# A fused two-layer mixture kernel on one core: phases of 3, 3 and 2 batches in the second mixture, and the second expert bias added once per batch

## What is computed

```python
x = x + 0.5 * L0_ffn(layernorm(x))     # mixture 1: top 2 of 8 experts per token
x = x + L0_attn(layernorm(x))          # 16 causal heads of 8 features, rotary
x = x + 0.5 * L0_ffn(layernorm(x))     # mixture 2, the same weights
x = x + 0.5 * L1_ffn(layernorm(x))     # 6-bit quantized 128x128 product + bias
x = x + L1_attn(layernorm(x))          # gated causal scan, then gated feed-forward
x = x + 0.5 * L1_ffn(layernorm(x))     # as above

# L0_ffn: combine[e] is the softmax gate of expert e for the token, 0 for six of the eight
h = relu(x @ w1 + bb1)                 # 128 -> 512
acc = acc + (h @ w2 + bb2) * combine[e]
```

## Time and profile before

| | |
|---|---|
| median of 3 runs | 953.89 us |
| the profiled execution | 953.64 us, of which the span from first to last instruction is 951.9 us |
| mean granted TensorE clock | 0.948 of full speed |
| busy of the span | PE 89%, DVE 64%, ACT 58%, POOL 70% |
| DMA | 127.65 MB, 134 GB/s |

### The profile page before, as it was taken

The page is one execution under the profiler, slowest core; times in us unless marked ns, Lnnn a source line. Parts: engine busy times, 40 slices in busy tenths (PEclk is TensorE's granted clock), DMA queues, the critical chain, the costliest instruction groups (busy, mean ns, idle before and its releaser), DMA issues.

```text
span 951.9 us, 23220 instructions
## 1 busy us (share of the span) xinstructions
PE 843.4 (89%) x7513; PEld 612.7 (64%) x7513; DVE 612.6 (64%) x1906; ACT 551.4 (58%) x1230; POOL 662.0 (70%) x846
## 2 busy tenths in 40 slices
PE   6379899989999999999999999999987998756894
PEld 3279798837665765665566655559965997344563
DVE  7620255674687977788979777865435335588775
ACT  4345444365568666675776667575763557735752
POOL 3789785998864378597734986971899874886432
PEclk8679899999999999998999999999999999878897
DMA  8878576736553434533443543325533771101000
GB/s 310 293 228 249 166 207 193 224 108 182 168 162 94 119 118 144 143 105 103 122 135 107 146 141 98 112 65 156 156 95 97 219 210 56 28 26 33 1 12 33
DMA packets 116280, 127.65 MB, mean 134 GB/s; under 512 B 14779, under 2 KB 84667, under 8 KB 116038
## 3 DMA queue, kind: packets, MB, share of 16 engines
q1 hardware_dynamic: 107974, 109.38, 39.4%
q0 software_dynamic: 8192, 16.79, 5.9%
HBM read 85.35 MB, written 40.39 MB: 132 GB/s over the span
## 4 chain that ended last, share of the span: by engine, by line
PE 41%; POOL 29%; DVE 15%; issue 7%; ACT 5%; DMA 2%; POOLq 0%; DVEq 0%; ACTq 0%
PE bank L801 38%; POOL z_scratch L1700 9%; POOL small L1691 9%; POOL yg L1713 4%; PE bank L813 4%; DVE sm_m L1324 3%; ACT P L1575 2%; POOL P L1735 2%; POOL sm_f L1675 1%; DMA yg<-y_scratch,pos 1%; DVE xs L1265 1%; POOL sm_p L1675 1%; DVE sm_f L1146 1%; POOL xs L1771 1%; ACT P L1488 1%
## 5 line engine op out<-in xcount | busy, mean ns | idle before, releaser
L1324 DVE TENSOR_REDUCE sm_m<-bank 128x4 f32<-128x512 f32 (+2 forms) x320 | 204.5, 683 | 37.8 <-PE bank L801 37.0
L1575 ACT ACTIVATE P<-bank 128x512 f32<-128x512 f32 x320 | 175.9, 601 | 60.1 <-PE bank L801 55.6
L801 PE MATMUL bank<-w2r,hb 128*128 x1360 | 188.0, 282 | 0.0
L801 PE MATMUL bank<-zt,wt 128*128 128x128 f32 x1360 | 182.9, 285 | 4.6 <-ACT zt L1518 2.9
L801 PEld LDWEIGHTS bank<-zt,wt 128*128 128x128 f32 x1360 | 167.3, 197 | 17.9 <-ACT P L1575 5.0
L1735 POOL TENSOR_SCALAR_AFFINE_SELECT P<-P 128x256 f32<-128x256 f32 (+1 forms) x320 | 115.5, 377 | 90.5 <-ACT P L1575 86.8
L801 PEld LDWEIGHTS bank<-w2r,hb 128*128 128x128 f32 x1360 | 165.6, 192 | 3.4 <-issue 1.6
L1700 POOL DMA_INDIRECT z_scratch<-zb,pos x128 | 134.2, 1048 | 45.7 <-issue 25.8
L1534 ACT ACTIVATE hb<-bank 128x512 f32<-128x512 f32 x170 | 101.3, 597 | 90.9 <-PE bank L801 90.5
L1691 POOL TENSOR_TENSOR small<-small 128x4 f32<-128x4 f32 x140 | 148.3, 1059 | 6.9 <-DVE pos L1247 3.6
L1713 POOL DMA_INDIRECT yg<-y_scratch,pos x128 | 130.8, 1022 | 23.9 <-issue 20.2
(11 more groups left out here) (221 smaller groups left out, 1362.5 us busy)
## 6 DMA issues: line engine op xcount, KB each, us to landing
wt<-w_scratch SPq DMA_DIRECT2D x170, 256.0 KB
zin<-z_scratch SPq DMA_DIRECT2D x82, 128.0 KB
y_scratch<-yt SPq DMA_DIRECT2D x82, 128.0 KB
q_scratch<-qpart SPq DMA_DIRECT2D x48, 128.0 KB
k_scratch<-kpart SPq DMA_DIRECT2D x48, 128.0 KB
Ks<-k_scratch SPq DMA_DIRECT2D x64, 96.0 KB
Qs<-q_scratch SPq DMA_DIRECT2D x64, 96.0 KB
z_scratch<-P SPq DMA_DIRECT2D x6, 512.0 KB, 7.0
```

The source lines that it names most:

```text
L801: return e.matmul(o, lhs, rhs, start=start, stop=stop, **kw)
L1324: e.tensor_reduce(to, of, AX.X, ALU.max, negate=True).then_inc(*d_max.step(i, f"m{s_}"))
L1575: e.activation(P[:, (2 * i + s_) % PR, :], shared("scor", i, 0, s_), ACT.Exp, scale=SCALE).then_inc(*a_sc.step(i, f"e{s_}"))
```

## The change

**The phases.** Mixture 2 is cut into batches 0-2, 3-5 and 6-7. The blocks of phases 3, 4, 5 become 31, 31, 23 instead of 23, 31, 31.

**The bias.** The bias matmul of each block goes, and with it the columns of the experts in `bias`. Instead, once per unit, a new stage `shift` adds gate-weighted biases to x. VectorE multiplies the two one-hot tables by their gates and adds them into `share` (128 tokens by 4 tiles x 8 experts), TensorE transposes it (32 by 128), ScalarE copies it to `sharet`, TensorE multiplies it by `b2d`, a 32 by 512 table that holds the 8 biases four times on its block diagonal, and VectorE adds the 128 by 512 result to x. `comb` waits for that addition. One more DMA loads `b2d`.

**The favours.** A table `FAVOUR` adds to `left` a number by stage and by phase or batch. The planner searches its order without them, in 6 rounds, and lays it out once more with them. So the order changes throughout.

```diff
-ORDER = [of(1, 0, 1), of(1, 2, 3, 4), of(1, 5, 6, 7), of(2, 0, 1), of(2, 2, 3, 4), of(2, 5, 6, 7)]
+ORDER = [of(1, 0, 1), of(1, 2, 3, 4), of(1, 5, 6, 7), of(2, 0, 1, 2), of(2, 3, 4, 5), of(2, 6, 7)]
-BIAS = (NE + 1) * 128
+BIAS = 128
+GR = 3
-PASSES = 8
+PASSES = 6
...
-    "bias": ("D1.4 D1.4 D1.0 D1.4",
+    "bias": ("D0.4 D0.3 D0.3 D0.3",
-    "res": ("P1 P1+0.2 A0.3+0.15 S0.5+4.5",
+    "res": ("P0.9 P0.9+0.2 A0.3+0.15 S0.5+4.5",
+    "shift": ("D0.6+0.15 P0.12+0.2 A0.26+0.15 P0.45+0.2 D0.6+0.15",
+            [(1, 2), (3, 4)], 1),
...
+FAVOUR = {
+    "head": {0: 4},
+    "scat": {4: -6, 5: 12},
+    "moe": {0: -4, 2: -12},
+    "att": {1: -4, 5: 20, 6: 30, 7: 30},
+    "comb": {2: -4, 3: -4, 5: -5},
+    "tail": {2: 4, 6: -5, 7: -5},
+}
...
     for _ in range(PASSES):
         rows, bank_of, end = forward(plan, queues, before, left)
-        if found is None or end < found[2]:
-            found = rows, bank_of, end
+        if found is None or end < found[0]:
+            found = end, left
         left = backward(plan, queues, before, rows)
-    rows, bank_of, _ = found
+    rows, bank_of, _ = forward(plan, queues, before, {x: v + favour(x[0], x[1]) for x, v in found[1].items()})
...
+            def shift(q):
+                o = take("shift", q, 1, a_shift.at(q, "t"))
+                w.wait_ge(l_first, 64)
+                w.wait_ge(*d_shift.at(q, "g"))
+                e.transpose(o[0:32, 0:128], share[:, q % GR, 0, :], ident[:, :]).then_inc(*t_shift.step(q, "t"))
+                yield
+                o = take("shift", q, 3, d_shift.at(q, "x"))
+                w.wait_ge(l_b2, 16)
+                w.wait_ge(*a_shift.at(q, "t"))
+                mm(o, sharet[:, :], b2d[:, :], True, True).then_inc(*t_shift.step(q, "y"))
+                yield
...
-                        mm(y, ones[:, :], bias[:, bass.DynSlice(at, 128)], j == 0, False, skip_group_check=True)
                         for c in range(NC):
-                            t = mm(y, hb[u % HB][:, c, :], w2[:, bass.DynSlice(at * 4 + 128 * c, 128)], False, c == NC - 1,
+                            t = mm(y, hb[u % HB][:, c, :], w2[:, bass.DynSlice(at * 4 + 128 * c, 128)], j == 0 and c == 0, c == NC - 1,
...
+            def shifted(q):
...
+                for k, name in enumerate("ab"):
+                    e.tensor_tensor(parts[:, k, :, :], oh[:, k, T, :], gate[:, b, k, :].unsqueeze(2).to_broadcast([128, 4, 8]), ALU.mult
+                                    ).then_inc(*d_shift.step(q, name))
+                w.wait_ge(*d_shift.at(q, "b"))
+                e.tensor_tensor(share[:, q % GR, 0, :], share[:, q % GR, 0, :], share[:, q % GR, 1, :], ALU.add
+                                ).then_inc(*d_shift.step(q, "g"))
+                yield
+                w.wait_ge(*t_shift.at(q, "y"))
+                x_ready(w, q)
+                x = xs[:, b, :, :]
+                e.tensor_tensor(x, x, blocks(shared("shift", q, 3)), ALU.add).then_inc(*d_shift.step(q, "x"))
```

More of the change, by code:

```diff
@@ L219, in follows @@
             return [("first", 0, 0)]
[L220 removed]
+        return [("route", OF_UNIT[u] - 1, 1), ("shift", PHASE[OF_UNIT[u]].unit - 1, 0)] if k == 9 else []
     if stage == "route":
@@ L273, in network @@
 def network():
-    counts = {"begin": 1, "first": 1, "xload": NB - 2, "zero": 1, "fill": 1, "late": 1, "later": 1, "sload": NE, "split": NE, "wquant": 1, "prep": 2 * NB, "route": PHASES, "scat": NTILE,
+    counts = {"begin": 1, "first": 1, "xload": NB - 2, "zero": 1, "fill": 1, "late": 1, "later": 1, "sload": NE, "split": NE, "wquant": 1, "prep": 2 * NB, "shift": 2 * NB, "route": PHASES, "scat": NTILE,
               "bias": 1,
@@ L1855 @@
     w2 = g["L0_ffn_W2"].reshape(NE, NC, 128, D).transpose(2, 0, 1, 3).reshape(128, NE, 512)
-    bias = np.concatenate([g["L0_ffn_b2"].reshape(-1), g["L1_ffn_bias"]])
+    b2d = np.zeros((4, NE, 4, D), np.float32)
+    for j in range(4):
+        b2d[j, :, j, :] = g["L0_ffn_b2"]
     arrays = {
```

59 lines of the change are left out of this document (47 added, 12 removed), and 2 rows, old and new, of the table STAGES.

## The result

The changed kernel takes 951.1 us (median of 20 runs), the kernel before 954.27 beside it: a ratio of 0.9965, 95% interval [0.9949, 0.9981]. The ratio leaves out one run of each kernel that took twice as long or more. On another chip later it was 0.9961 [0.9943, 0.998]. That is faster, by a third of a per cent, and within the 1% that the prediction called the same. 937 us was forecast.

A forecast was written before the change was run, and what follows sets the result against it. TensorE was taken as bound from 56 to 797 us, then a chain through phase 5's gathers. Last copy 800.1, last addition 853.6, plus 76.4 gives 930.0; 5.5 for room and 1.7 around the span give 937 us, range 919 to 959.

The forecast's parts named there:

- Batch 7 out of attention: Exit of batch 7 from the attention in TensorE's order: predicted to move from 652.8 to 659.4 us.
- -13.1 for the bias matmuls: TensorE ahead of batch 7's out-projection: 125 bias matmuls fewer, at 0.105 us each by starts, take 13.1 us off.
- +8.7 and +1 for the shifts: Ahead of batch 7's exit: nine bias shifts not hidden at the start add 8.7 us on TensorE, VectorE's additions 1 us.
- part 3: Favours pull the attention of batches 5 to 7 ahead; counted in the orders, with bounds of -8 and +15 us.
- The last stretch: From the last addition to x to the end: 80.4 us before, 76.4 predicted, some six feed-forward steps of batch 5 moving ahead.
- 5.5 for missing room: Before the last addition: some 50 us of VectorE work at 88% density needs 59 us in 53, so 5.5 us added.
- 16 gathers instead of 24: Phase 5's gathers: 15 steps of 2.56 us, 38.4 us, so the last addition ends at 853.6 instead of 871.5 us.
- Part 1: Bias change on TensorE: 170 matmuls removed, 17.9 us, against 15.5 us added over 16 units; net 2.4 us saved.
- Part 2: Phases 3, 3, 2: same 85 blocks, batch 7 out at 659.4, last expert copy unmoved at 800.1, fewer gathers at the end.
- B: Rival, chance 0.11: POOL becomes the bound in the attention, 38 us of row calls delaying selects; slower, 975 us.
- A: Rival, chance 0.19: the tail is bound by work, not gathers; density stays 71%, 149 us after 800.1, 951 us, no change.
- C: Rival, chance 0.13: added products cost half, a fuller tail keeps the clock up, and the room is found; 924 us.

The follow-up runs named there:

- e1: Kernel before in its own order, the 170 bias matmuls of the expert blocks left out: 952.17 us, ratio 0.9993 to the kernel before.
- e2: Changed kernel in its own order, the shift stage emptied: 944.98 us, ratio 0.9916 to the kernel before.
- e4: Kernel before with the new per-unit bias alone, old phases, no favours: 954.8 us, ratio 1.0007 to the kernel before.
- e16: Kernel before, old phases and per-block bias, with favours found by a search in the planner: 935.55 us, ratio 0.9813 to the kernel before.
- e12: Changed kernel with old phases, searched favours and the planner told 1.05 us per bias product: 940.84 us, second run 938.15; ratios 0.9821, 0.9828 to the kernel before.
- e17: e12 with the shift stage empty, run beside e12's second run: 938.79 us against 938.15.
- e3: Kernel before with the new phases 3, 3, 2 alone, old bias, no favours: 965.98 us, ratio 1.0131 to the kernel before.
- e13: Changed kernel with its new phases, searched favours and the planner told 1.05 us per bias product: 942.69 us, ratio 0.9851 to the kernel before.
- e5: Changed kernel without its favours: 961.71 us, ratio 1.0082 to the kernel before.
- e6: Changed kernel with the old phases 2, 3, 3, its bias and favours kept: 976.07 us, ratio 1.0236 to the kernel before.
- e15: Changed kernel, causal selects of batches 3 and 4 over 32 columns instead of 128 or 256, order unchanged: ratio 0.9898 to the kernel before.
- e10: Changed kernel with expert blocks of phases 2 and 3 held back by up to 20 and 30 us: 977.88 us, ratio 1.0254 to the kernel before.

## Why the prediction was wrong

**The step that failed** is "Batch 7 out of attention: 5 more blocks, +10.0; 125 bias matmuls fewer, -13.1; nine shifts not hidden at the start, +8.7; VectorE +1. So 652.8 becomes 659.4 us." It was 684.2 and 680.0 us in two profiles, 21 to 25 us later. The part that it names:

- *-13.1 for the bias matmuls* was about half that: e1, which takes away 120 of them ahead of batch 7, moved its exit by 5.5 us instead of 12.6. The duration of 0.105 us was right; that a busy engine's work comes out of the time was not. In the changed kernel it is the part ahead of 195 us that is missing, 54 matmuls or 5.7 us: at 195 us both kernels have done the output products of 54 blocks.
- *+8.7 and +1 for the shifts*: e2 against the changed kernel, 671.4 against 680.0 to 684.2, is 9 to 13 us. At most 3 us short, of which the product's 1.05 us instead of 0.86 is 1.7 over nine. The price was taken from two products in a row; the lone one of the kernel before shows 1.06.
- *What was not in it*: what an order does to TensorE's idleness and clock. I counted 125 instead of 120 hidden steps ahead of batch 7, and didn't look at how they lie between its steps. The windows from 195 us to batch 7's exit, two of the kernel before, one of the changed kernel, three of its second profile:

```profile
195.00:400.00 205.00, 196.54 (x2092) 126.87 (x2092) 150.54 (x399) 135.33 (x279) 140.29 (x225) 0.99 0.48 137
195.00:652.80 457.80, 440.77 (x4700) 279.00 (x4697) 352.89 (x985) 304.63 (x633) 323.36 (x521) 0.99 0.44 125
...
195.00:684.20 489.20, 467.00 (x4759) 292.37 (x4758) 360.73 (x976) 307.62 (x644) 318.94 (x517) 0.97 0.43 122
...
195.00:400.00 205.00, 197.16 (x2002) 124.75 (x2003) 160.55 (x424) 129.53 (x272) 118.15 (x199) 0.98 0.43 123
400.00:480.00 80.00, 68.12 (x731) 35.09 (x731) 65.76 (x180) 47.15 (x96) 68.75 (x106) 0.94 0.39 108
195.00:680.00 485.00, 461.44 (x4757) 291.15 (x4756) 361.69 (x976) 307.50 (x644) 317.61 (x517) 0.98 0.43 123
```

TensorE is idle for 22.2 and 23.6 us instead of 17.0. For the clock I estimate busy time times what is missing to 1.00, in 195 to 400 and 400 to 480 us (behind them it is 1.00): 197.26 x 0.04 + 69.19 x 0.11 = 15.5 us in the changed kernel and 197.16 x 0.02 + 68.12 x 0.06 = 8.0 in its second profile, against 196.54 x 0.01 + 77.21 x 0.04 = 5.1. So 5.2 and 6.6 us more of idleness, of which the sum had 1, and some 10 and 3 us of clock. With 5.7 for the bias matmuls and 1.7 for the products that is 22 of the 25 us and 16 of the 21. The rest stays open, and each figure comes from one or two profiles whose exits lie 4 us apart.

My part 3 put a bound of +15 on the order "from the 17 us that PE is idle in 195 to 653". That was the idleness of the old order and bounds nothing in a new one. And I took a window in which TensorE is full for one in which its work sets the time.

**From batch 7's exit on** the prediction held, in part by luck. To the last copy 134.0 us (140.7 predicted), to the first gather 8.5 (7.8), to the last addition 45.8 (45.7). The last stretch was 81.4 us where I had 76.4. I had added 5.5 for missing room, but ahead of the last addition, where it was not needed; that the sum of the two, 81.9, fits is luck. One reading was wrong without harm: VectorE is not the busiest engine over all the gathers, GpSimd is, with 51.1 us against 44.5 in 805 to 865 us. The 16 gathers instead of 24 win what was said of them.

**The parts.** Part 1 (net 2.4 us saved) was right in that it is about nothing, by e4, e16 against e12's second run, and e17; but for another reason than the sum: in e1 and e17 work taken out of TensorE, 12.8 us of it in e17, doesn't move the end. It is not so in every order: in the changed kernel's own, emptying the stage (e2) brings 5 to 6 us. Part 2 (phases, 16 us) is right for the tail alone; by itself it loses 12 us (e3), and in a searched order it is worth nothing that can be told (e13 against e12). Part 3, "no instruction of their own", with bounds of -8 and +15, is the largest: 11 us between e5 and the changed kernel, the other way in e6, 16 to 18 us between the kernel before and e12 or e16.

**The rivals.** B named the right place, the attention in 195 to 653 us with more row calls among its selects, and had the wrong limit: POOL is 86% busy in 400 to 480, but lightening it (e15) brought phase 3's blocks forward by 2 to 6 us only. Its signs did not come: from 195 us to the exit POOL is 65% busy (318.94 of 489.20 us), not above 80, and TensorE is idle for 22 to 24 us, not more than 25, with no wait for GpSimd among the longest. The delay was 21 to 25 us, not its 38, and the gain in the tail covered it. A's time, 951, is the one measured, but that is luck. Its sign, an early last addition with the end still near 950, did not come (872.5, not 855), and from the last copy to the end are 135.7 us where A needs 149. C's higher clock came while the gathers run (0.91 in 818 to 873 us, 0.84 before) and was given back behind them (0.85, 0.87 before).

**What stays open.** Idleness and clock over 195 to 684 us were not separated; the runs change both at once, and two profiles of one kernel split them differently. That the order decides is shown: e6 and e12 have the same phases and the same bias handling and take 976 and 941 us, and e5 differs from the changed kernel by nothing but its favours. Which feature of an order does is not: the row without blocks fits e3, e5 and e6, but not e10 and e13, and e4 has short rows (24, 33) and gains nothing. Why e10 loses 27 us is read from its milestones and was not tested.
